# The transposed mask of a windowed attention moved from TensorE to GpSimd, with two of four transposed slots placed earlier

## What is computed

```
B, S, D = 8, 1024, 256        # 16 heads of 16
q = apply_rope(proj(Wq, bq)) * Dh ** (-0.5)
k = apply_rope(proj(Wk, bk))
v = proj(Wv, bv)
scores = jnp.einsum('bhqd,bhkd->bhqk', q, k)
rel = idx[None, :] - idx[:, None]
blocked = (rel > 0) | (rel < -WINDOW)          # WINDOW = 128
scores = jnp.where(blocked[None, None], -jnp.inf, scores)
probs = jax.nn.softmax(scores, axis=-1)
out = jnp.einsum('bhqk,bhkd->bhqd', probs, v)  # then projected, added to x, layer-normed
```

## Time and profile before

| | us |
|---|---|
| median of 3 runs | 2849.27 |
| lowest, highest | 2844.29, 2855.34 |
| the profiled execution | 2839.36 |
| its span (first to last instruction) | 2837.5 |
| TensorE busy in the span | 2315.9 (82%) |
| VectorE, ScalarE, GpSimd busy | 1485.0, 886.6, 677.7 |

### The profile page before, as it was taken

The page is one execution under the profiler, slowest core; times in us unless marked ns, Lnnn a source line. Parts: engine busy times, 40 slices in busy tenths (PEclk is TensorE's granted clock), DMA queues, the critical chain, the costliest instruction groups (busy, mean ns, idle before and its releaser), DMA issues. The chain is left out here.

```text
span 2837.5 us, 44896 instructions
## 1 busy us (share of the span) xinstructions
PE 2315.9 (82%) x18544; PEld 1432.9 (50%) x18544; DVE 1485.0 (52%) x2615; ACT 886.6 (31%) x1257; POOL 677.7 (24%) x404
## 2 busy tenths in 40 slices
PE   2899999999999985677675598894598898889896
PEld 1455555555555455565563266553355555555553
DVE  2445555555555544455454165547556756766662
ACT  0233333333333333333341121220143333334332
POOL 4121112221111201131431433433102113202212
PEclk7899999999999997898888799997699999999997
DMA  6455664555565404675676210102443244235230
GB/s 144 93 105 111 118 123 99 114 113 104 114 117 115 98 24 148 221 257 178 212 240 208 78 60 30 60 30 66 143 129 97 78 144 144 73 103 159 84 91 16
DMA packets 227353, 329.19 MB, mean 116 GB/s; under 512 B 15072, under 2 KB 164944, under 8 KB 226896
## 3 DMA queue, kind: packets, MB, share of 16 engines
q1 hardware_dynamic: 224336, 325.68, 43.0%
q10 hardware_dynamic: 2816, 0.65, 0.1%
HBM read 197.71 MB, written 127.93 MB: 115 GB/s over the span
## 5 line engine op out<-in xcount | busy, mean ns | idle before, releaser
L1678 ACT ACTIVATE l1f_probs<-l1f_slot 128x1024 f32<-128x1024 f32 x240 | 240.6, 1022 | 423.1 <-PE l1f_slot L1851 252.3
L518 DVE TENSOR_REDUCE l0a_rowmax<-l0a_slot 128x4 f32<-128x1024 f32 (+1 forms) x256 | 293.4, 1156 | 128.4 <-PE l0a_slot L631 125.5
L461 ACT ACTIVATE l0a_probs<-l0a_slot 128x1024 f32<-128x1024 f32 (+1 forms) x256 | 248.4, 971 | 338.0 <-PE l0a_slot L621 189.0
L1741 DVE TENSOR_REDUCE l1f_rowmax<-l1f_slot 128x1 f32<-128x1024 f32 x240 | 287.6, 1219 | 100.5 <-PE l1f_slot L1837 100.3
L1851 PE MATMUL l1f_slot<-l1f_Qs,l1f_Ks 128*128 128x256 f32 x960 | 184.5, 319 | 42.9 <-DVE l1f_rowmax L1741 16.8
L1851 PEld LDWEIGHTS l1f_slot<-l1f_Qs,l1f_Ks 128*128 128x128 f32 x960 | 141.6, 200 | 113.2 <-ACT l1f_probs L1678 30.3
L1837 PE MATMUL l1f_slot<-l1f_Ks,l1f_Qs 96*128 96x512 f32 x480 | 170.7, 449 | 29.2 <-DMA l1f_Qs<-kq_rows 12.7
L421 POOL TENSOR_TENSOR l0a_turned<-l0a_turned 128x512 f32<-128x512 f32 x32 | 40.7, 1272 | 560.8 <-DVE l0a_turned L504 560.8
L621 PE MATMUL l0a_slot<-l0a_mask,l0a_ident 128*128 128x512 bf16 (+1 forms) x512 | 150.4, 376 | 25.7 <-issue 23.4
L1796 PE MATMUL l1f_os<-l1f_probs,l1f_V 128*32 128x256 f32 x1920 | 165.8, 398 | 1.8 <-ACT l1f_probs L1678 0.9
L563 PE MATMUL l0a_O<-l0a_probs,l0a_V 128*32 128x128 f32 x3840 | 156.5, 279 | 10.6 <-issue 10.6
(11 more groups left out here) (190 smaller groups left out, 4069.3 us busy)
## 6 DMA issues: line engine op xcount, KB each, us to landing
expert_outputs<-l0f_inter SPq DMA_DIRECT2D x64, 512.0 KB, 3.7
l0f_wide<-expert_outputs SPq DMA_DIRECT2D x32, 1024.0 KB, 10.2
l0a_Qs<-qk_rows SPq DMA_DIRECT2D x96, 256.0 KB, 7.8
l0a_Ks<-qk_rows SPq DMA_DIRECT2D x96, 256.0 KB, 14.8
l1f_Ks<-kq_rows SPq DMA_DIRECT2D x48, 512.0 KB, 6.7
qk_rows<-l0a_hi SPq DMA_DIRECT2D x32, 512.0 KB, 2.8
qk_rows<-l0a_lo SPq DMA_DIRECT2D x32, 512.0 KB, 4.2
l0f_f<-in_dram SPq DMA_DIRECT2D x32, 512.0 KB, 5.1
```

The source lines that it names most:

```text
L461: exp_ready.by(act.activation(probs[:, t % 2, HG * g:HG * g + HG, 0:reach, :], s[:, :, 0:reach, :], ACT.Exp, scale=SCALE))
L518: max_ready.by(dve.reduce_max(rowmax[:, t, :, 2 * g:2 * g + 2], s[:, :, :, first:2 * P], AX))
L1678: exp_done.by(act.activation(probs[:, half, u - FIRST[i], :], s[:, :], ACT.Exp, scale=SCALE))
L1741: max_done.by(dve.reduce_max(rowmax[:, 2 * u + t:2 * u + t + 1], s[:, :], AX))
```

## The change

The table `maskT` and its load are gone, and with them TensorE's two mask matmuls in each `tr`. In their place ScalarE copies the slot unmasked into `probs` (signal `copied`), GpSimd writes -1e30 over the blocked triangle in place with `affine_select`, once for each of the two neighbouring tiles (signal `cut`), and ScalarE takes the exponential from `probs` into `probs` (new entry `exp`). In the last tile of a sequence there is one tile, and one selection. The order of a stage is new as well: the first `tr` of a stage stands behind the second `nat`, the second `tr` behind the third `nat`, the third behind `oT`, and the fourth among the rest; the `exp` of group g comes right behind the `tr` of group g + 1, and the last at the start of the next stage.

```
@@ the list of steps @@
     for i in range(BT):
         on, tn = divmod(i + 3, BT)
         ot, tt = divmod(i + 1, BT)
-        steps += merged([(0, "pv", NHG * i + g) for g in range(NHG)], [(on, "nat", NHG * tn + g) for g in range(NHG)],
-                        begun.get(i, []))
-        steps += [(0, "oT", i)]
-        steps += merged([(ot, "tr", NHG * tt + g) for g in range(NHG)], [(on, "maxT", tn), (on, "place", tn), (0, "back", i)], front[i])
+        pv, nat = [(0, "pv", NHG * i + g) for g in range(NHG)], [(on, "nat", NHG * tn + g) for g in range(NHG)]
+        tr = [(ot, "tr", NHG * tt + g) for g in range(NHG)]
+        row = [(0, "exp", NHG * i + NHG - 1)] + merged(pv[:2], nat[:2]) + tr[:1] + merged(pv[2:3], nat[2:3]) + tr[1:2]
+        row += merged(pv[3:], nat[3:]) + begun.get(i, []) + [(0, "oT", i)] + tr[2:3]
+        row += merged([(on, "maxT", tn), (on, "place", tn), (0, "back", i)], tr[3:], front[i])
+        for step in row:
+            steps += [step] + ([(ot, "exp", step[2] - 1)] if step[1] == "tr" and step[2] % NHG else [])
@@ readers of a slot @@
-            return [{"nat": (max_ready, n + 1), "maxT": (maxT_ready, n + 1), "tr": (exp_ready, n + 1),
+            return [{"nat": (max_ready, n + 1), "maxT": (maxT_ready, n + 1), "tr": (copied, n + 1),
@@ GpSimd @@
+                if kind == "tr":
+                    t, g = i // NHG, i % NHG
+                    copied.wait(pool, X, i + 1)
+                    alone_here = bool(n and t == BT - 1)
+                    for a, sign in enumerate((1,) if alone_here else (1, -1)):
+                        part = probs[:, t % 2, HG * g:HG * g + HG, a, :]
+                        pool.affine_select(part, part, [[0, HG], [sign, P]], ALU.is_ge, BLOCKED, base=0, channel_multiplier=-sign)                            .then_inc(cut.sem, 2 if alone_here else 1)
@@ ScalarE @@
-                    exp_ready.by(act.activation(probs[:, t % 2, HG * g:HG * g + HG, 0:reach, :], s[:, :, 0:reach, :],
-                                                ACT.Exp, scale=SCALE))
+                    copied.by(act.copy(probs[:, t % 2, HG * g:HG * g + HG, 0:reach, :], s[:, :, 0:reach, :]))
+                if kind == "exp":
+                    t, g = i // NHG, i % NHG
+                    part = probs[:, t % 2, HG * g:HG * g + HG, 0:1 if n and t == BT - 1 else 2, :]
+                    cut.wait(act, X, 2 * i + 2)
+                    exp_ready.by(act.activation(part, part, ACT.Exp, scale=SCALE))
@@ TensorE, kind "nat" or "tr" @@
-                    mask_ends = bool(kind == "tr" and g % 2)
...
-                    if not mask_ends:
-                        add_mask()
+                    if kind == "nat":
+                        for half in range(2):
+                            mm(o[:, half, :, reach, :], ident16[:, :], mask[:, reach, :].unsqueeze(1).broadcast_to([P, 2, wide, P]),
+                               start=True, stop=False, skip_group_check=True)
...
-                    if mask_ends:
-                        last = add_mask()
```

More of the change, by code:

```diff
@@ L263, in window_attention_layer @@
     SCALE = float(DH) ** -0.5
+    BLOCKED = -1e30
     CH = D // P
@@ L287, in window_attention_layer @@
         mask = sb("mask", [P, 2, P], bf16)
-        maskT = sb("maskT", [P, 2, P], bf16)
         wq = sb("wq", [P, CH, D]); wk = sb("wk", [P, CH, D]); wv = sb("wv", [P, CH, D]); wo = sb("wo", [P, CH, D])
@@ L327, in window_attention_layer @@
         placed = [signal(f"placed{t}", BT, 16) for t in range(2)]
-        exp_ready = signal("exp_ready", BT * NHG); pv_done = signal("pv_done", BT * NHG)
+        copied = signal("copied", BT * NHG); exp_ready = signal("exp_ready", BT * NHG); cut = signal("cut", 2 * BT * NHG); pv_done = signal("pv_done", BT * NHG)
         oT_ready = signal("oT_ready", BT); recip_ready = signal("recip_ready", BT); ao_ready = signal("ao_ready", BT)
@@ L338, in window_attention_layer @@
         schedule.signals(filled, reader)
-        NCONST = 12 + 2 * HR
+        NCONST = 11 + 2 * HR
         NSETUP = 8
@@ L351, in _ @@
                 sp.dma_start(dst[:, :], src).then_inc(consts, 16)
-            for dst, src in ((mask, mask_in), (maskT, maskT_in)):
-                sp.dma_start(dst[:, :, :], src.rearrange("p (a n) -> p a n", a=2)).then_inc(consts, 16)
+            sp.dma_start(mask[:, :, :], mask_in.rearrange("p (a n) -> p a n", a=2)).then_inc(consts, 16)
             for dst, src in ((as_given[0], wq_in), (as_given[1], wk_in), (wv[:, :, :], wvT), (wo[:, :, :], woT)):
@@ L404, in _ @@
         def _(pool):
-            for s in (biased, rot_ready, lo_ready):
+            for s in (biased, rot_ready, lo_ready, cut):
                 s.start(pool)
@@ L436, in _ @@
         def _(act):
-            for s in (xT_ready, hi_ready, exp_ready, oT_ready, aoT_ready, *placed):
+            for s in (xT_ready, hi_ready, copied, exp_ready, oT_ready, aoT_ready, *placed):
                 s.start(act)
@@ L609, in piece @@
                         reach = slice(0 if tile else 1, 2)
-                        rows, table, left, right = ROWS, mask, Qs, Ks
+                        rows, left, right = ROWS, Qs, Ks
                         moving = slice(P * (tile - 1 + reach.start), P * tile + P)
@@ L613, in piece @@
                         reach = slice(0, 2 if tile < NT - 1 else 1)
-                        rows, table, left, right = ROWS + 1, maskT, Ks, Qs
+                        rows, left, right = ROWS + 1, Ks, Qs
                         moving = slice(P * tile, P * (tile + reach.stop))
                     wide = reach.stop - reach.start
-                    mask_ends = bool(kind == "tr" and g % 2)
-                    def add_mask():
+                    if kind == "nat":
                         for half in range(2):
-                            at_end = mm(o[:, half, :, reach, :], ident16[:, :],
-                                        table[:, reach, :].unsqueeze(1).broadcast_to([P, 2, wide, P]),
-                                        start=not mask_ends, stop=bool(mask_ends), skip_group_check=True)
-                        return at_end
-                    if not mask_ends:
-                        add_mask()
+                            mm(o[:, half, :, reach, :], ident16[:, :], mask[:, reach, :].unsqueeze(1).broadcast_to([P, 2, wide, P]),
+                               start=True, stop=False, skip_group_check=True)
                     for j in range(2):
@@ L631, in piece @@
                             last = mm(o[:, half, j, reach, :].rearrange("p a q -> p (a q)"), left[r, 2 * g + j, here],
-                                      right[r, 2 * g + j, moving], start=mask_ends and not j, stop=not mask_ends,
+                                      right[r, 2 * g + j, moving], start=kind == "tr", stop=True,
                                       skip_group_check=True, tile_position=(HALF * half, 0))
-                    if mask_ends:
-                        last = add_mask()
                 if kind == "maxT":
```

## The result

| | before | with the change |
|---|---|---|
| median, us | 2846.78 (4 runs, 2838.96 to 2855.34) | 2918.45 (4 runs, 2912.15 to 2924.40) |
| ratio | | 1.0258, 95% interval 1.0227 to 1.0289 |
| span of the profiled execution, us | 2837.5 | 2910.3 |

What follows compares the result with a forecast made beforehand. The prediction took TensorE to bound the first layer. 7 pairs of blocks at +8.4 us gave 59, plus 4 at the edges: +63 on 2849.3, so 2912 us, with a range of 2833 to 2985.

Steps and rivals of the forecast that it cites:

- TensorE bounds the layer: First layer: TensorE busy 801.95 of 860 us; masks leaving save 8.5 us per heavy block (one leading into a full tile).
- The check beside it: Check on the mask work: 416 mask matmuls were busy 124.1 us, taken as about 13 blocks.
- A selection at 1.27 us: GpSimd's price c for one selection, taken from its joins of the same shape, between bounds of 0.61 and 1.48 us.
- the walk: Step-by-step timing of a block by the new order: a pair takes 131.8 us at c = 1.27, 122.1 at 0.65.
- The waits of the chain: Slot, copy, two selections, exponential: some 13 us of new TensorE waits in a heavy block, the largest 3.3 us at `proj`.
- I cost them at nothing: Second signal at each selection and earlier issue of `place` behind an exponential: a stage of slack each, no cost.
- The clock, at most 14 us in all: TensorE's clock may fall at the wait for `proj` in heavy blocks: 1.8 us a time, at most 14 us.
- fast selections: Rival: c up to 0.73 is not slower, 2839 us at the low end; c near 0.9 gives 2869; chance 0.30 in two parts.
- GpSimd as the bound: Rival: a selection costs 1.48 us or more, so GpSimd's work and queue hold the time: 2969 us; chance 0.22.
- TensorE as the bound: Rival: TensorE stays the bound and the 116 us gain less a few waits remains: 2740 to 2800 us; chance 0.05.
- The clock rival: Rival: long waits such as that for `proj` lower TensorE's clock, at most 14 us; within the range, no separate chance.
- The signs named: What the later profile would show if right, such as blocks 64 to 68 us apart, or wrong, such as blocks under 58.

Runs made afterwards that it cites:

- e5: The changed kernel with every GpSimd selection done twice, the second waiting for the first: 3064.54 us, ratio 1.0775.
- e4: The changed kernel without GpSimd's selections, the exponential waiting for its copy alone (plan timed only, weights not the reference's): 2907.90 us, ratio 1.0217.
- e7: Mask on GpSimd in the order of before, exponential straight from the slot, GpSimd then zeroing the blocked triangles (plan timed only): 2840.31 us, ratio 0.9993.
- e2: The kernel before with only the change's new order of steps, masks staying on TensorE: 2931.76 us, ratio 1.0302.
- g1: The changed kernel with `v` moved ahead of the last transposed slot of stage 3 and `aoT` behind it: 2938.06 us, ratio 1.0326.
- f1: The changed kernel with idle matmuls put ahead of TensorE's longest waits: 2895.45 us, ratio 1.0188.
- f3: The changed kernel with `pv`, `nat` and `tr` in the order of before, plus idle matmuls ahead of its longest waits: 2881.20 us, ratio 1.0129.
- g3: The changed kernel with the tail of each stage reordered, plus idle matmuls ahead of the waits left: 2842.51 us, ratio 0.9994.
- g4: The kernel of g3 with eleven more idle matmuls in stage 0: 2826.10 us, ratio 0.9931.

## Why the prediction was right, and where it was not

**TensorE bounds the layer; its mask work is 8.5 us a heavy block.** The reading of before is right, and the masks left. TensorE's busy time in the layer fell by 60 us instead of some 120, because the matmuls that stayed ran slower. The check beside it was loose: 416 full-size mask matmuls are those of about 15 blocks (32 in a heavy one, 24 in a light one), not 13, or 8.3 us for a mean block.

**A selection at 1.27 us.** Wrong; it took 0.639. It lay beside the bound from below, GpSimd's copy at 0.61 us. The step that failed is the choice "near the arithmetic rows and far from the copy": neither the two-input join nor the TENSOR_SCALAR priced this instruction. The Trainium skill, "GPSIMD Engine Reference", section 4.1 Engine selection, has one input run at roughly line rate; the selection's 0.639 us agrees with that, the TENSOR_SCALAR row of 1.48 does not. This term was 9.7 us a pair too dear by the walk (131.8 against 122.1), some 73 us in all. e5 took 3065 us at 1.37 us a selection; on the line from the change (selections 0.61 us apart, 2918 us) to e5, an estimate, the assumed 1.27 would have given some 3045 us. So with its own price the forecast would have been far too low.

**The waits of the chain.** Right in sum near the real price, 22.4 against 22.6 us, and some 3 us too many at the doubled one, in part by luck, since the items differ. The list of the change: maxima 7.16 us a pair, the turned k 2.46, the copies ahead of `v` 2.67 and of `proj` 1.20, xT 1.48, as the walk named them. It left out the wait of the first `pv` for V (3.12 a pair), and that of a `nat` for the maximum of the slot's last tenant (1.46). That the waits on copies come from ScalarE's queue whatever GpSimd does was shown by e4 (no selection, no shorter waits) and fits e7 (one pass, 62 us less).

**"I cost them at nothing": `place` and its slack of a stage.** Wrong, though cheap in the change itself (0.40 us a pair ahead of a `tr`, with no releaser named). The transfer needs 11 to 12 us in stage 3, so there is no slack once the first `tr` stands early: 3.49 us a pair in e2, 9.37 in g1.

**The clock, at most 14 us in all.** Wrong, the largest miss of the sum. The step that failed is the search for a wait as long as 2.43 us; waits of 0.3 to 1.3 us close together did it three times a block. The bookkeeping gives 10.9 us a pair, 76 us over seven pairs, of which filling recovered 23 in the change; how much of the rest is the clock's stays open. This and the price of the selection cancelled: the "fast selections" case at 2839 us plus the clock's 76 is 2915, beside the measured 2918. That the total came out right is luck.

**The rivals.** Fast selections was the case that held, but "not slower" below c = 0.73 did not follow, because the clock was not in it. GpSimd as the bound did not occur even at twice the price: e5 has it busy 576 of 860 us, though its time was above the 2969 of that case. TensorE as the bound did not occur. The clock rival was the right mechanism, with a size of up to five times what I gave it.

**The signs named.** Blocks of 64 to 68 us: met. AFFINE_SELECT of 1.1 to 1.4 us and GpSimd busy by 550 to 650 us more: not met (0.639, and 970.4 - 677.7 = 293). TensorE's busy time down by 120 us in the layer: not met (60); its idle time up by more than the busy time fell: met (130). The sign for "wrong" said that a selection near 0.6 comes with blocks of 60 to 62 us; they took 65 to 68.

## What to carry to other kernels

Work taken off the bounding engine is gained only where something else can follow at once; here 15.1 us of new waits a pair stood against 16.2 us of work taken off. Price the clock with the waits: here several waits of about 1 us in a row were enough to lose it, and a handful of idle matmuls in them is a cheap experiment that tells at least part of what it costs. A right total proves no term: run the kernel near the assumed price (here the doubled selection) and see whether it lands there.

## What the runs showed of the hardware

- GpSimd's selection over 128x512 f32 in place takes 0.639 us, against 1.484 for its TENSOR_SCALAR with one constant over the same shape.
- TensorE's granted clock went to 0.50 for some 3.4 us after a stretch of 4 us in which it was busy 1.72 us, none of the single waits above 1.2 us. In the same block a wait of 1.56 us by itself left the clock at 1.00. The Trainium skill, "TensorE: Matmul & The Clock Gate", section HAM oscillation, warns of long gaps above all; here rows of short ones did it.
- For a transfer of 4 KB issued right behind six of 256 KB, and ahead of two of 512 KB on another queue, the matmul that needs it began 11 to 12 us after the end of the issue (e2, g1).
- Idle matmuls ahead of waits raised the granted clock from 0.91 to 0.97 (f1), 0.93 to 0.99 (f3), 0.90 to 0.95 (g3) and 0.95 to 0.99 (g4), with 23, 21, 37 and 16 us less.
